# A recurrence of 512 steps on one core: the candidate's scan takes three terms, its bias is added on TensorE, and the state's high half is copied at another place

## The reference, cut to what matters

```python
def cell(h, x):
    gi = x @ W_ih + b_ih
    gh = h @ W_hh + b_hh
    i_r, i_z, i_n = jnp.split(gi, 3, axis=-1)
    h_r, h_z, h_n = jnp.split(gh, 3, axis=-1)
    r = jax.nn.sigmoid(i_r + h_r)
    z = jax.nn.sigmoid(i_z + h_z)
    n = jnp.tanh(i_n + r * h_n)
    h_new = (1.0 - z) * n + z * h
    return (h_new, h_new)
xs = jnp.swapaxes(inputs, 0, 1)
_, hs = jax.lax.scan(cell, initial_state, xs)
...
x = x + _L0_ffn_ref(_L0_cond_ref(cond_2048, x, ...), ...)
x = x + _L1_ffn_ref(_L1_cond_ref(x, cond_2048, 1, 1), ...)
```

## Time and profile before

| what | before |
| --- | --- |
| median of three runs | 1917.95 us |
| the profiled execution's own time | 1916.69 us |
| its span from first to last instruction | 1914.9 us |
| TensorE busy (matmuls) | 1705.6 us, 89% |
| VectorE busy | 1378.1 us, 72% |
| ScalarE busy | 764.4 us, 40% |
| GpSimd busy | 312.7 us, 16% |
| first and last matmul group of the recurrence (L581) | 31.5 and 1698.6 us |

### The profile page before, as it was taken

The page is one execution under the profiler, slowest core; times in us unless marked ns, Lnnn a source line. Parts: engine busy times, 40 slices in busy tenths (PEclk is TensorE's granted clock), DMA queues, the critical chain, the costliest instruction groups (busy, mean ns, idle before and its releaser), DMA issues.

```text
span 1914.9 us, 90635 instructions
## 1 busy us (share of the span) xinstructions
PE 1705.6 (89%) x38754; PEld 1097.7 (57%) x38754; DVE 1378.1 (72%) x6318; ACT 764.4 (40%) x2706; POOL 312.7 (16%) x592
## 2 busy tenths in 40 slices
PE   6888888878889999988899999988899999988995
PEld 5666666655555565555555555555555666554442
DVE  6888888887877777777777777777777777763222
ACT  5555566543333343332333434332333343323332
POOL 2222222221211011121211111121211111021001
PEclk9999999999999999999999999999999999999997
DMA  7445344345225464426135556334145454259993
GB/s 251 156 158 199 126 165 181 152 181 177 88 104 202 161 260 159 158 84 211 59 129 186 213 191 221 109 107 162 58 178 185 178 212 175 95 171 371 377 342 88
DMA packets 113220, 334.25 MB, mean 175 GB/s; under 512 B 41880, under 2 KB 42032, under 8 KB 100400
## 3 DMA queue, kind: packets, MB, share of 16 engines
q1 hardware_dynamic: 107696, 311.68, 45.0%
q0 software_dynamic: 5120, 16.78, 2.7%
HBM read 263.09 MB, written 65.31 MB: 171 GB/s over the span
## 4 chain that ended last, share of the span: by engine, by line
PE 49%; DVE 36%; ACT 7%; issue 6%; DMA 1%; DVEq 0%; SPq 0%; POOL 0%; ACTq 0%
PE bank_g L581 15%; PE bank L748 11%; PE bank_g L587 11%; DVE xt L1148 9%; DVE pre L1150 5%; DVE na L1156 5%; DVE xt L1152 5%; ACT seq_h L880 5%; DVE seq_n L1153 4%; DVE hs_early L1162 4%; PE bank_g L594 3%; PE bank L619 2%; PE bank L744 2%; PE bank L765 2%; DVE wih L1366 1%
## 5 line engine op out<-in xcount | busy, mean ns | idle before, releaser
L1459 POOL COPY hxs<-hs 128x32 f16<-128x32 f16 x512 | 236.0, 461 | 1372.4 <-DVE hs L1167 1372.2
L581 PE MATMUL bank_g<-whh,hs_early 128*32 128x256 f16 x8192 | 318.5, 275 | 153.1 <-DVE hs_early L1162 140.5
L880 ACT ACTIVATE rz<-pre 128x32 f32<-128x32 f32 x512 | 119.2, 233 | 732.2 <-DVE pre L1150 731.3
L581 PEld LDWEIGHTS bank_g<-whh,hs_early 128*32 128x32 f16 x8192 | 172.6, 96 | 350.5 <-DVE hs_early L1162 343.1
L1148 DVE STREAM_TRANSPOSE xt<-bank_g 128x256 f32<-128x256 f32 x512 | 230.5, 450 | 181.2 <-PE bank_g L587 174.4
L594 PE MATMUL bank_g<-whh,hs 128*32 128x128 f16 x16384 | 320.1, 219 | 6.8 <-issue 6.7
L587 PE MATMUL bank_g<-whh,hs 128*32 128x256 f16 x8192 | 313.9, 273 | 1.3 <-issue 0.8
L748 PE MATMUL bank<-wm,wih 128*128 128x512 f16 x1272 | 308.5, 381 | 4.7 <-ACT wih L880 2.5
L594 PEld LDWEIGHTS bank_g<-whh,hs 128*32 128x32 f16 x16384 | 282.4, 97 | 10.2 <-issue 8.5
L880 ACT ACTIVATE seq_h<-na 128x16 f32<-128x16 f32 x512 | 111.7, 218 | 257.4 <-DVE na L1156 257.4
L587 PEld LDWEIGHTS bank_g<-whh,hs 128*32 128x32 f16 x8192 | 182.8, 96 | 45.6 <-DVE hs L1167 3.7
(11 more groups left out here) (183 smaller groups left out, 1951.2 us busy)
## 6 DMA issues: line engine op xcount, KB each, us to landing
wm<-moe_split SPq DMA_DIRECT2D x53, 1536.0 KB
wm<-moe_split SPq DMA_DIRECT2D x53, 1024.0 KB, 6.3
wm<-moe_split SPq DMA_DIRECT2D x53, 512.0 KB
wm<-in_w_moe SPq DMA_DIRECT2D x16, 1536.0 KB, 6.6
moe_split<-wm SPq DMA_DIRECT2D x16, 1536.0 KB, 6.5
y_rows<-wih SPq DMA_DIRECT2D x60, 256.0 KB, 4.0
wih<-x_rows SPq DMA_DIRECT2D x58, 256.0 KB, 7.9
xr<-in_x SPq DMA_DIRECT2D x16, 512.0 KB, 7.0
```

Of the source, the lines that this page charges most:

```text
L581: mm(bank_g[0][32 * j:32 * j + 32, 0:2 * P], early_cols[:, 4 * B * k:4 * B * k + 32], whh[:, 1, k, at:at + 2 * P], start=(k == 0), stop=False)
L880: return nc.scalar.activation(dst, src, func, **kw)
L1459: Q.tensor_copy(hxs[:, par, :, :, :, col].rearrange("p s k b -> p s (k b)"), hs_new).then_inc(S["h_kept"], 1)
```

## The change

Three things change, with what they need at the start:

1. The n product is transposed so that high and low part of each output lie in one array with the input's part, `xt_n[:, 2]` with 3 elements for each output. The sum of L1153 is gone. The scan goes over groups of three with factors 0, 1 and r. The state's columns are laid out in groups of 8 (high half in column 4, low half in column 5).
2. The bias is written to TensorE's bank in front of the n product: 4 matmuls with a contraction over two rows (partitions 64 and 65, high and low half of the bias) and a stationary operand of 32 columns.
3. The copy of the high half still stands behind the second scan, but waits for the first one's end only (`h_hi`); the low half waits for the second one (`h_new`).

At the start, the three constants are loaded ahead of `w_hh`. GpSimd builds two diagonal arrays from the bias, TensorE sums them (2 matmuls of 512 columns) and ScalarE copies the result to the two rows.

```diff
-        hs = sb("hs", [P, 2 * K * B + 2 * B, 2], F16)
-        hs_early = sb("hs_early", [P, 2 * K * B + 2 * B, 2], F16)
-        xt = sb("xt", [P, G3, 64], F32)
+        hs = sb("hs", [P, K * B, 8], F16)
+        hs_early = sb("hs_early", [P, K * B, 8], F16)
+        xt = sb("xt", [P, 2 * K, 64], F32)
+        xt_n = sb("xt_n", [P, 4, K * B, GROUP], F32)
...
+        bias_rows = slice(P // 2, P // 2 + 2)
+        bias_n, bias_to = brow[bias_rows, 0, 0:D], brow[bias_rows, 0, D:D + 8 * B]
...
-        early_scan = hs_early[:, 0:2 * K * B, 0]
+        early_scan = early_cols.rearrange("p (c s) -> p s c", s=4)[:, 0]
+        rows_n = xt_n[:, :, :, 0:2].rearrange("p q g s -> p g q s")
+        seq_n = xt_n[:, 2]
...
+            for dst, src in ((idt[:, :], ident), (iote[:, :], iota_e), (iotf[:, :], iota_f)):
+                sp.dma_start(dst, src).then_inc(S["const_in"], 16)
             for q in range(3):
                 sp.dma_start(part_of(wm32[1], q), part_of(w_hh, q)).then_inc(whh_in[q], 16)
-            for dst, src in ((idt[:, :], ident), (iote[:, :], iota_e), (iotf[:, :], iota_f)):
-                sp.dma_start(dst, src).then_inc(S["const_in"], 16)
...
                 i.then_inc(S["gates_mm"], 1)
+                if t == 0:
+                    pe.wait_ge(S["bias_row"], 1)
+                for j in range(K):
+                    mm(bank_g[1][32 * j:32 * j + 32, 0:P], bias_to, bias_n[:, j * P:(j + 1) * P],
+                       start=True, stop=False)
...
-                                   start=(k == 0 and w == 0), stop=(k == K - 1 and w == 1))
+                                   start=False, stop=(k == K - 1 and w == 1))
...
+            pe.wait_ge(S["bias_diag"], 2)
+            for w in range(2):
+                i = mm(bank_l[1][:, :], bias_at[:, w], bias_d[:, w].rearrange("p k n -> p (k n)"),
+                       start=(w == 0), stop=(w == 1))
+            i.then_inc(S["bias_mm"], 1)
             pe.wait_ge(S["whh_split"], 3)
...
+            act.wait_ge(S["bias_mm"], 1)
+            run(bias_n.rearrange("p (j m c) -> p m j c", j=K, m=K),
+                bank_l[1][bias_rows, :].rearrange("p (m j c) -> p m j c", m=K, j=K), ACT.Copy).then_inc(S["bias_row"], 1)
...
-                link(V.transpose(rows[:, 2 * K:], bank_g[1][:, 0:P].rearrange("p (m c) -> p m c", c=32)))
-                link(V.tensor_reduce(seq_n[:, :, 0:1].rearrange("p (k b) o -> p k (b o)", b=B), terms[:, 2 * K:],
-                                     AX, ALU.add))
+                link(V.transpose(rows_n, bank_g[1][:, 0:P].rearrange("p (g q s) -> p g q s", q=4, s=2)))
...
-                link(V.tensor_tensor_scan(pairs["hh"], pairs["omz"], pairs["seq_h"], 0.0, ALU.mult, ALU.add))
+                V.tensor_tensor_scan(pairs["hh"], pairs["omz"], pairs["seq_h"], 0.0, ALU.mult, ALU.add
+                                     ).then_inc(S["h_new"], 1)
+                dve.wait_ge(S["h_hi"], t + 2)
                 dve.wait_ge(S["h_kept"], t + 1)
                 V.tensor_copy(hs_hi, early_hi)
+                dve.wait_ge(S["h_new"], t + 1)
                 tt_(hs_lo, hh[:, :, 1], early_hi, ALU.subtract).then_inc(S["h_ready"], 1)
...
-            step(ts_(ext[:, 2 * K:], bh[:, 2 * K:3 * K].unsqueeze(2).to_broadcast([P, K, B]), PS, None, ALU.mult))
+            step(V.memset(rz[:, 0:K * B, 1:GROUP - 1], 1.0))
+            step(V.memset(bias_to, 0.0))
+            step(V.memset(bias_to[:, 4:8 * B:8], AS))
...
+            Q.tensor_scalar(bias_w[:, :], bh[:, 2 * K:], WS, None, ALU.mult).then_inc(S["bias_two"], 1)
...
+            for w in range(2):
+                Q.tensor_tensor(bias_d[:, w], idt[:, :].unsqueeze(1).to_broadcast([P, K, P]),
+                                bias_s[:, w].unsqueeze(2).to_broadcast([P, K, P]), ALU.mult
+                                ).then_inc(S["bias_diag"], 1)
```

More of the change, by code:

```diff
@@ L29 @@
 LORA_SCALE = 32.0 / RANK
+GROUP = 3
 AS, WS = 16.0, 64.0
@@ L317, in adaln_ffn_kernel @@
             setup_dve zero_set const_set warm wih_hi whh_hi b2_hi b1_mm b1_hi l0_hi wih_split whh_split b1_split b2_split l0_split moe_lo moe_hi
-            h_hi h_ready gates_mm now_in rz_pre n_pre rz_done n_done gru_chain h_kept
+            bias_two bias_diag bias_mm bias_row bias_sum h_hi h_new h_ready gates_mm now_in rz_pre n_pre rz_done n_done gru_chain h_kept
             x_hi x_split gi_mm gi_done grid_chain grid_a grid_r grid_hi
@@ L885, in gates_now @@
                 now = gi[:, col // TB, :, :, col % TB:col % TB + 1]
-                run(ext[:, 0:2 * K].unsqueeze(3), now[:, 0:2 * K], ACT.Copy)
-                run(seq_n[:, :, 1:2].rearrange("p (k b) o -> p k b o", b=B), now[:, 2 * K:], ACT.Copy
+                run(ext.unsqueeze(3), now[:, 0:2 * K], ACT.Copy)
+                run(seq_n[:, :, GROUP - 1:GROUP].rearrange("p (k b) o -> p k b o", b=B), now[:, 2 * K:], ACT.Copy
                     ).then_inc(S["now_in"], 1)
@@ L891, in gru_rz @@
                 act.wait_ge(S["rz_pre"], t + 1)
-                run(rz[:, :, 1:2].rearrange("p a o -> p (a o)"), pre[:, :, :].rearrange("p m b -> p (m b)"),
+                run(r_new.rearrange("p a o -> p (a o)"), pre[:, :, :].rearrange("p m b -> p (m b)"),
                     ACT.Sigmoid, scale=1 / PS).then_inc(S["rz_done"], 1)
@@ L896, in gru_n @@
                 act.wait_ge(S["n_pre"], t + 1)
-                run(seq_h[:, :, 0:1], na[:, :, 1:2], ACT.Tanh, scale=1 / PS).then_inc(S["n_done"], 1)
+                run(seq_h[:, :, 0:1], n_new, ACT.Tanh, scale=1 / PS).then_inc(S["n_done"], 1)
             def gru(t, col):
@@ L1147, in gru @@
                 dve.wait_ge(S["gates_mm"], t * 2 + 1)
-                link(V.transpose(rows[:, 0:2 * K], bank_g[0][:, 0:2 * P].rearrange("p (m c) -> p m c", c=32)))
+                link(V.transpose(rows, bank_g[0][:, 0:2 * P].rearrange("p (m c) -> p m c", c=32)))
                 dve.wait_ge(S["now_in"], t + 1)
-                V.tensor_reduce(pre[:, :, :], terms[:, 0:2 * K], AX, ALU.add).then_inc(S["rz_pre"], 1)
+                V.tensor_reduce(pre[:, :, :], terms, AX, ALU.add).then_inc(S["rz_pre"], 1)
                 dve.wait_ge(S["gates_mm"], t * 2 + 2)
-                link(V.transpose(rows[:, 2 * K:], bank_g[1][:, 0:P].rearrange("p (m c) -> p m c", c=32)))
-                link(V.tensor_reduce(seq_n[:, :, 0:1].rearrange("p (k b) o -> p k (b o)", b=B), terms[:, 2 * K:],
-                                     AX, ALU.add))
+                link(V.transpose(rows_n, bank_g[1][:, 0:P].rearrange("p (g q s) -> p g q s", q=4, s=2)))
                 dve.wait_ge(S["rz_done"], t + 1)
@@ L1506, in _ @@
             Q.memset(warm, 0.0).then_inc(S["warm"], 1)
+            Q.memset(bias_at, 0.0).then_inc(S["bias_sum"], 1)
+            pool.wait_ge(S["bias_sum"], 1)
+            for w in range(2):
+                Q.memset(bias_at[:, w, P // 2 + w:P // 2 + w + 1], 1.0)
+            pool.wait_ge(S["bias_in"], 16 * 6)
+            pool.wait_ge(S["const_in"], 16 * 3)
+            Q.tensor_scalar(bias_w[:, :], bh[:, 2 * K:], WS, None, ALU.mult).then_inc(S["bias_two"], 1)
+            pool.wait_ge(S["bias_two"], 1)
+            Q.tensor_copy(bias_s[:, 0], bias_w[:, :]).then_inc(S["bias_two"], 1)
+            pool.wait_ge(S["bias_two"], 2)
+            Q.tensor_tensor(bias_s[:, 1], bias_w[:, :], bias_s[:, 0], ALU.subtract).then_inc(S["bias_two"], 1)
+            pool.wait_ge(S["bias_two"], 3)
+            for w in range(2):
+                Q.tensor_tensor(bias_d[:, w], idt[:, :].unsqueeze(1).to_broadcast([P, K, P]),
+                                bias_s[:, w].unsqueeze(2).to_broadcast([P, K, P]), ALU.mult
+                                ).then_inc(S["bias_diag"], 1)
             for n in ("h_kept", "d_out"):
```

34 lines of the change are left out of this document (19 added, 15 removed).

## The result

The changed kernel takes 1964.38 us (median of four, 1961.81 to 1968.02) against 1917.97 us beside it: ratio 1.0241, interval 1.0221 to 1.0261. That is +46 us where +25 was forecast. The direction and the mechanism were right; the time lies 7 us above the range. The profiled execution's span went from 1914.9 to 1963.4 us, +48.5.

The account below looks back on a forecast made before the run. The recurrence's round trip was taken as the bound, beside expert tiles by 0.04 to 0.15 us only. Terms -12 + 36 + 0 + 1.5 = +25.5 us on 1916.7 gave 1942.2, hence 1943 us; range 1908 to 1957, own range 1930 to 1955.

Parts of the forecast that it names:

- TensorE is all but full beside expert tiles; the chain is the bound by 0.04 to 0.15: Expert-tile steps: room ahead of L581 is 0.15 us in four of six steps, 0.04 in the two with L744.
- A change of shape costs 0.10, two of them and the work 0.27: 2-row bias matmuls between L587 and L594: 0.27 us more TensorE time each step, of which 0.06 is work.
- no change of shape: Rival: bias matmuls follow L587 like any others, 0.06 us more TensorE time a step; 1885 us, chance 0.13.
- half of it: Rival: one of the two changes of shape is hidden, 0.16 us a step; 1916 us, chance 0.06.
- The chain is shorter by 0.094: L1152 to scan L1156: dropping L1153 saves 0.13 us, the longer scan costs 0.03; 0.094 less each step.
- Strides of ScalarE's copies and of `keep` change, not their element counts: 0: ScalarE's copies and `keep` in each step: changed strides cost nothing, both engines being idle over 1 us a step.
- a chain that isn't shorter: Rival: transpose L1152 in its new pattern takes over 0.1 us more, so the gain is lost; 1963 us, chance 0.05.
- 128 steps beside input products: -12 us: First stage: room 0.67 us against 0.27 + 0.09, so the chain's gain stays, 128 x -0.094 = -12 us.
- 270 tile steps: +36: Steps beside expert tiles: 180 grow by 0.12 us, 90 by 0.23, together 42; less 6 gives +36 us.
- The 6 that I took off: Expert-tile steps already longer than 3.2 us swallow added time while TensorE waits in the filler: 30 x 0.2 = 6 us.
- The start, +1.5: Before step 0: small loads, VectorE steps, two matmuls and a ScalarE copy add 1.5 us, bounds 0 and 7.
- the cover of 0.05 for the late L594: L594 starting 0.27 us later mostly hides: L1156 could go at 807.03, ahead of the sigmoid's 807.08; 0.05 left.

Follow-up runs that it names:

- rows128: Changed kernel with its four bias matmuls over all 128 rows of the array instead of 2: 1921.21 us, ratio 1.0021.
- before_plus_4tiny: Kernel before the change with four more matmuls a step, 128 rows by 32 columns, each over 8 moving columns: ratio 1.0104.
- bias_by_act: Changed kernel without bias matmuls in the steps; ScalarE copies the bias, computed once at the start, into the bank each step: 0.9865, repeated 1894.28 us, 0.9876.
- bias_one_mm: Changed kernel with its four bias matmuls replaced by one of 128 rows by 128 columns: 1952.09 us, ratio 1.018.
- no_bias_old_copy: Changed kernel without bias matmuls (bias left out), the high half's copy waiting for the second scan's end as before: 1895.67 us, ratio 0.9888.

## Why the prediction was right in kind and wrong in size

- *TensorE is all but full beside expert tiles; the chain is the bound by 0.04 to 0.15.* Right: the rooms are 0.150, 0.133 and 0.047 (medians of 90 steps each); after, L593 follows the filler without room, and TensorE's share of the chain is 74%.
- *A change of shape costs 0.10, two of them and the work 0.27.* Right: from the second group to the n product it is 0.704 instead of 0.437 (medians), 0.267 more; one change less gave 0.11 a step, a change of columns alone gave the same 0.27, and without a change 43 us were gone. The rivals *no change of shape* and *half of it* are out. The first one's price, 1885 us, was too low as well: rows128, which meets its condition, takes 1921, since eight instructions more cost what no term had. The rule of the Trainium skill, page "TensorEngine Tiling (Array Packing)", section "Key Properties", that a change of tiling mode drains TensorE, agrees with these 0.267 us; that was the case that no row of before had.
- *The chain is shorter by 0.094.* The scan and the sigmoid's release came as forecast. 0.062 was measured. The step that failed here is "Strides of ScalarE's copies and of `keep` change, not their element counts: 0", which also overlooked the sigmoid, tanh and state scan; their rows are 27 ns longer. That the stride does it is read from what changed, not tried. The rival *a chain that isn't shorter* is out: the transpose takes 326 ns on average instead of 307, within its cover, and the period beside input products is 3.14. That its price, 1963 us, is nearly the measured time is chance.
- *128 steps beside input products: -12 us.* Measured -1.5. 4 of the 10.5 are the smaller gain. The other 6.5 are a term the sum didn't have: 5.3 are the 8 steps in which TensorE waits for a packet of instructions, and before_plus_4tiny ties these waits to the number of instructions; about 1 is not explained.
- *270 tile steps: +36.* Measured +46.8. The median steps are 3.329, 3.344 and 3.430 (90 each), against 3.20: 90 x (0.126 + 0.142 + 0.228) = 45. The sum had 42 from room 0.15 in 180 steps, where half of them have 0.133. The 6 that I took off were wrong: steps that were long before (13 us above the medians) are matched by 16 us above the medians after. The added time came on top of them instead of vanishing in their waits.
- *The start, +1.5, and the cover of 0.05 for the late L594*: +2.3, and the cover held.

The step that failed, then, is the size of two terms. The tile steps' was +36 and measured +47, mainly since the 6 us of "swallowed" time don't exist. The first stage's was -12 and measured -1.5, since wider strides were put at nothing and eight more instructions in each step had no term at all. The range was too narrow since all its bounds came from durations, and none from the instructions.

## What to carry to other kernels

Before a small matmul goes between two large groups, look at the rows on either side: if rows or columns of the array differ, two changes of shape come with it, here 0.21 us beside 0.06 of work. Its neighbours' shape takes that away, but not the price of the added instructions (1.5% here). Better was to let an idle engine write the bank first and let the matmuls add to it; in bias_by_act matmuls had written the bank once at the start, and none behind them opens it anew (`start=True`). And read the room of the engine that isn't the bound stage by stage: 0.67 us in one stage and 0.04 in another make the same 0.27 free or dear.

## What the runs showed of the hardware

- A change of the array's shape costs TensorE 0.10 to 0.11 us: 128 rows by 32 columns to 2 by 32 and back, or to 128 by 128 and back, made 0.267 and 0.265 us, some 0.06 of it work (after, bias_one_mm); four matmuls of the same shape made 0.056 (rows128).
- Eight instructions more in each step on TensorE cost 1.0% of the kernel before whether the matmuls move 128 or 8 columns, and two cost 0.7%. With 77,500 instructions on TensorE and its weight loads there was no gap inside a block in the first 128 steps of six profiles, with 78,500 and more there was in all eleven.
- TensorE's instructions come in packets of 16,384 bytes, 256 of them. The first one of a packet starts 1.2 to 1.7 us behind its landing where TensorE had to wait; the gaps are 0.2 to 2.2 us long and can stand in the middle of like matmuls, wherever a packet's end falls.
- ScalarE's sigmoid on 32 elements takes 247 ns instead of 233 when it writes every third element instead of every second; VectorE's subtraction of 16 elements into every eighth f16 0.22 us instead of 0.19 into every fourth (no_bias_old_copy against before).
- ScalarE writes 128x128 f32 to a bank in 0.26 us, and matmuls add to what it wrote (bias_by_act).
